# Mask rows moved from ScalarE to VectorE, and a new order of work in the gated-attention layer of an eight-layer kernel

## The reference

```python
# cross attention 0 and 3, masked
sim = jnp.where(mask[:, None, None, :], sim, max_neg)
attn = jax.nn.softmax(sim, axis=-1)
...
# feed-forward 0, "gated attention"; rw: [b, t, 16] gates from _gating
rw = _gating(hidden_states, sim_matrix, gates)
q = jnp.einsum('bte,bted->btd', rw, jnp.einsum('btc,ecd->bted', hidden_states, q_proj))
k = ...  # the same with k_proj
v = ...  # the same with v_proj
scores = jnp.where(causal, jnp.einsum('bqd,bkd->bqk', q, k) * scale, -jnp.inf)
attn = jnp.einsum('bqk,bkd->bqd', jax.nn.softmax(scores, axis=-1), v)
mixed = attn[:, :, None, :] * rw[..., None]
return jnp.einsum('bted,edc->btc', mixed, o_proj)
```

## Time and profile before

| what | us |
| --- | --- |
| median of 3 runs | 3174.82 |
| lowest, highest run | 3174.57, 3177.18 |
| the profiled execution, its own time | 3177.18 |
| its span in the profile | 3175.4 |
| layer 0 attention, about | 0 to 348 |
| gated attention, about | 348 to 965 |
| layer 3 attention, about | 2358 to 3055 |

### The profile page before, as it was taken

How to read it: one execution, slowest core, us unless ns; L and a number is a source line. 1 busy time by engine, 2 the same in 40 slices (tenths; PEclk the granted TensorE clock), 3 DMA queues, 4 the chain that set the end, 5 groups by cost and what they waited for, 6 DMA issues and landing times. The chain is left out here.

```text
span 3175.4 us, 91385 instructions
## 1 busy us (share of the span) xinstructions
PE 2974.0 (94%) x35250; PEld 2314.1 (73%) x35250; DVE 2237.6 (70%) x6007; ACT 1577.7 (50%) x2929; POOL 1200.9 (38%) x1402
## 2 busy tenths in 40 slices
PE   7999799999998999689988999999989999999978
PEld 6888455555557888556667888888877888888854
DVE  6777666666645666677777777777767777777755
ACT  6777221111215777366663333333336777677746
POOL 6776100000005776644430000000016676667643
PEclk9999899999998999989998999999999999999989
DMA  5000266656650000011103333323320000000001
GB/s 166 10 11 5 87 189 186 169 163 189 179 148 9 11 10 8 2 61 26 23 16 99 102 104 97 96 97 107 108 64 12 8 10 10 7 10 10 8 1 54
DMA packets 111033, 212.23 MB, mean 67 GB/s; under 512 B 18769, under 2 KB 30609, under 8 KB 110353
## 3 DMA queue, kind: packets, MB, share of 16 engines
q1 hardware_dynamic: 110352, 209.19, 22.4%
q10 hardware_dynamic: 512, 0.92, 0.1%
HBM read 198.50 MB, written 5.77 MB: 64 GB/s over the span
## 5 line engine op out<-in xcount | busy, mean ns | idle before, releaser
L349 PE MATMUL ps<-parts 128*128 128x512 f32 (+2 forms) x1568 | 624.0, 398 | 30.0 <-DVE parts L1014 18.3
L350 PE MATMUL ps<-parts 128*128 128x512 f32 (+2 forms) x1568 | 565.2, 360 | 0.0
L351 PE MATMUL ps<-parts 128*128 128x512 f32 (+2 forms) x1568 | 564.5, 360 | 0.0
L319 POOL TENSOR_TENSOR rstd<-mv,eps 128x4 f32<-128x4 f32 x112 | 23.2, 208 | 1220.2 <-DVE mv L302 1220.0
L1934 ACT ACTIVATE work<-ps 128x512 f32<-128x512 f32 x272 | 162.6, 598 | 455.0 <-PE ps L351 454.8
L349 PEld LDWEIGHTS ps<-parts 128*128 128x128 f32 (+1 forms) x1568 | 299.3, 191 | 101.0 <-ACT work L846 26.2
L351 PEld LDWEIGHTS ps<-parts 128*128 128x128 f32 (+1 forms) x1568 | 298.6, 190 | 47.3
L350 PEld LDWEIGHTS ps<-parts 128*128 128x128 f32 (+1 forms) x1568 | 300.7, 192 | 21.0
L562 POOL TENSOR_TENSOR work<-work 128x512 f32<-128x512 f32 x256 | 266.9, 1043 | 128.2 <-DVE work L984 128.2
L1900 PEld LDWEIGHTS ps<-early,work 128*128 128x128 f32 x2176 | 281.3, 191 | 30.2 <-DVE work L1991 11.4
L1900 PE MATMUL ps<-early,work 128*128 128x128 f32 x2176 | 289.0, 276 | 8.1 <-DVE x L2098 8.1
(11 more groups left out here) (297 smaller groups left out, 6259.6 us busy)
## 6 DMA issues: line engine op xcount, KB each, us to landing
work<-gate_rows SPq DMA_DIRECT2D x128, 512.0 KB, 5.6
work<-expert_rows SPq DMA_DIRECT2D x512, 128.0 KB, 2.9
work<-gate_rows SPq DMA_DIRECT2D x128, 256.0 KB, 7.1
work<-in_ctxT SPq DMA_DIRECT2D x72, 192.0 KB, 2.4
out<-x SPq DMA_DIRECT2D x16, 256.0 KB, 2.3
work<-work SPq DMA_DIRECT2D x224, 16.0 KB
work<-work SPq DMA_DIRECT2D x16, 128.0 KB, 2.3
early<-in_l0f_w SPq DMA_DIRECT2D x1, 1536.0 KB, 8.2
```

The lines of the kernel that those rows point to most:

```text
L349: T.matmul(out, lh, rh, start=True, stop=False)
L350: T.matmul(out, lh, rl, start=False, stop=False)
L351: return T.matmul(out, ll, rh, start=False, stop=True)
```

## The change

It has three parts. (1) `mask_rows` goes from ScalarE to VectorE, as a `tensor_scalar` of the same 128x256 values: for the first unit just ahead of the first `shift`, and for each next unit at step 2, between `sums` and `shift`. (2) In the loop of the gated layer, PE runs `router(g + 2)` in slot 1, ahead of `scores(g)`, not in slot 0, and `turn_gates(g + 2)` behind `project(g + 1, 5)` in slot 5, not behind `attend(g)` in slot 4. VectorE runs `weight` one slot ahead of PE, not two; `mask` and `normalise` come ahead of the `weight` of their slot; and the three batches of `routing(g + 2)` are in slots 2 to 4, not 1 to 3. In the prologue VectorE makes two products of group 0, not four, ahead of the routing of group 1; ScalarE's copy for `null_values` comes ahead of the first `gate_exp`, and `squares(1)` behind the copy for `spectral_weight`. (3) The gates go through two DRAM tensors in turn, not through one with a place for each group, and `rows_out` waits until the reads of two groups before have landed.

```diff
--- before.py
+++ after.py
@@ -862,10 +862,6 @@
                 act.wait_ge(sub_ready, n + 1)
                 A.activation(pr[t % 2], sc[t % 2], ACT.Exp, scale=1.0 if masked else scale).then_inc(exp_ready, 1)
 
-            def mask_rows(un):
-                tiles = mask[:, bass.ds(un.g * TG, TG), :]
-                A.activation(nm[un.u], tiles, ACT.Copy, bias=NEG, scale=-NEG).then_inc(nm_ready, 1)
-
             def weights_high(dst, src, parts):
                 for p in range(passes):
                     cols = slice(p * HP * DH, (p + 1) * HP * DH)
@@ -890,9 +886,6 @@
             if boot:
                 act.wait_ge(boot.ctx1, 16)
             A.activation(ch[1][0:DC, :], c.ctx01[0:DC, 0 if null else 1, :], ACT.Copy).then_inc(high, 1)
-            if masked:
-                act.wait_ge(mask_in, 16)
-                mask_rows(first)
             for j in range(NJ):
                 take_query(first, j, j % 2)
             if null:
@@ -923,9 +916,6 @@
                             A.activation(r0T[0:2 * HP, :], c.ps[0:2 * HP, 4, :], ACT.Copy).then_inc(r0t_ready, 1)
                         act.wait_ge(o_ready, n + 1)
                         A.activation(oT.rearrange("p j b q -> p b j q"), ps_o, ACT.Copy).then_inc(ot_out, 1)
-                        if masked and t == 0 and not end:
-                            need(act, s_read, n)
-                            mask_rows(un.next())
                         if turns(u, t, last):
                             take_hT(un.g + 1 if null else un.k + 2)
                         if not (end and t == TG - 1):
@@ -954,6 +944,10 @@
 
         @block.vector
         def _(ve):
+            def mask_rows(un):
+                tiles = mask[:, bass.ds(un.g * TG, TG), :]
+                V.tensor_scalar(nm[un.u], tiles, 1.0, -NEG, ALU.subtract, ALU.mult).then_inc(nm_ready, 1)
+
             def shift(n, un, t):
 
                 if masked and t == 0:
@@ -1036,6 +1030,9 @@
             context_low(second)
             ve.wait_ge(ht_full, 1)
             norm.scale(ve, 1)
+            if masked:
+                ve.wait_ge(mask_in, 16)
+                mask_rows(first)
             shift(0, first, 0)
             if null:
                 norm.take_moments(ve, 1, 1)
@@ -1064,6 +1061,8 @@
                             elif not (isinstance(it, int) and it == 0):
                                 add(it * 2 - 1)
                         if t < 2 or not end:
+                            if t == 2 and masked:
+                                mask_rows(un.next())
                             if boot and isinstance(it, int) and it == 0 and u == 0 and t == 3:
                                 ve.wait_ge(s_ready, n + 3)
                                 boot.vector_second(ve, c.ps[:, 3, S:S + NE0])
@@ -2139,7 +2138,7 @@
     ps_q, ps_v = [c.ps[:, i, :] for i in range(2)], [c.ps[:, 2 + i, :] for i in range(2)]
     ps_s, ps_m, ps_a, acc = (c.ps[:, 4 + i, :] for i in range(4))
     dup = c.w["dup"]
-    rows = nc.dram_tensor("gate_rows", [n * NE0, GT], FP).ap()
+    rows = [nc.dram_tensor(f"gate_rows{i}", [NE0, GT], FP).ap() for i in range(2)]
     norm = Norm(c, "f0_ln", hn)
     sem = lambda s: c.sem("f0_" + s)
     ht_full, ht_out, r_ready, r_read, n2_ready, rn_ready, gexp, rw_ready, link, wt_full, wt_out, rows_in = (
@@ -2161,21 +2160,23 @@
             def rows_out(g, u):
 
                 sp.wait_ge(wt_out, g + 1)
-                sp.dma_start(rows[bass.ds(g * NE0, NE0), :], rwT[u][0:NE0, :]).then_inc(rows_in, 16)
+                if not (isinstance(g, int) and g < 2):
+                    sp.wait_ge(split_in, (g - 1) * NM * 32)
+                sp.dma_start(rows[u], rwT[u][0:NE0, :]).then_inc(rows_in, 16)
                 sp.wait_ge(rows_in, g * 16 + 16)
 
             def spread_wide(g, u, p):
 
                 if not (isinstance(g, int) and g == 0 and p < NW):
                     sp.wait_ge(hw_ready, g * NP + (p - NW + 1) if p >= NW else g * NP - (NW - 1 - p))
-                sp.dma_start(wide[p % NW], rows[bass.ds(g * NE0 + 2 * p, 2), :].unsqueeze(0).broadcast_to((P, 2, GT))).then_inc(wide_in[p % NW], 16)
+                sp.dma_start(wide[p % NW], rows[u][2 * p:2 * p + 2, :].unsqueeze(0).broadcast_to((P, 2, GT))).then_inc(wide_in[p % NW], 16)
 
             def spread_split(g, u, i):
 
                 if not (isinstance(g, int) and g == 0):
                     sp.wait_ge(mixed_ready, g * NM - (NM - 1 - i))
                 for e in range(2):
-                    src = rows[bass.ds(g * NE0 + 4 * i, 4), :].rearrange("(j e) k -> e j k", e=2)[e:e + 1, :, :]
+                    src = rows[u].rearrange("(j e) k -> e j k", e=2)[e:e + 1, 2 * i:2 * i + 2, :]
                     sp.dma_start(split[i][e * DH:(e + 1) * DH, :, :], src.broadcast_to((DH, 2, GT))).then_inc(split_in, 16)
 
             sp.dma_start(dft, d["dft"]).then_inc(dft_in, 16)
@@ -2340,17 +2341,17 @@
                             project(g + 1, 1 - u, s)
                         if s == 0:
                             values(g)
-                            if left(g + 2):
-                                router(g + 2, u)
                         if s < 2 and left(g - 1):
                             back(g - 1, 2 + s)
                         if s == 1:
+                            if left(g + 2):
+                                router(g + 2, u)
                             scores(g)
                         if s == 3:
                             turn_probs(g)
                         if s == 4:
                             attend(g)
-                        if s == 4 and left(g + 2):
+                        if s == 5 and left(g + 2):
                             turn_gates(g + 2, u)
                         if s >= 6:
                             back(g, s - 6)
@@ -2402,13 +2403,13 @@
             take_hT(0, 0), squares(0)
             act.wait_ge(freq_full, 1)
             A.activation(freq.rearrange("p n w -> p (n w)"), c.ps[:, 4, 0:2 * P], ACT.Copy).then_inc(freq_out, 1)
-            gate_exp(0), take_gates(0, 0)
-            take_hT(1, 1), squares(1)
             act.wait_ge(nv_full, 1)
             A.activation(c.w["l3_nwo"][:, :, :].rearrange("p b c -> p (b c)"), c.ps[0:16, 7, 0:2 * D], ACT.Copy).then_inc(nv_out, 1)
+            gate_exp(0), take_gates(0, 0)
+            take_hT(1, 1)
             act.wait_ge(spec_full, 1)
             A.activation(c.w["l1f_g"][:, :], c.ps[:, 6, 0:P], ACT.Copy).then_inc(spec_out, 1)
-            gate_exp(1), take_gates(1, 1)
+            squares(1), gate_exp(1), take_gates(1, 1)
 
             def body(it):
                 for u in range(2):
@@ -2536,15 +2537,14 @@
                 routing(0, 0, part)
             ve.wait_ge(n2_ready, TG)
             norm.vector(ve, 1)
-            for p in range(NHW):
-                weight(0, 0, p)
+            weight(0, 0, 0), weight(0, 0, 1)
             for part in range(11):
                 routing(1, 1, part)
             ve.wait_ge(n2_ready, 2 * TG)
             norm.vector(ve, 2)
-            for p in range(NHW, NP):
+            for p in range(2, NP):
                 weight(0, 0, p)
-            weight(1, 1, 0), weight(1, 1, 1)
+            weight(1, 1, 0)
             ve.wait_ge(spec_out, 1)
 
             def body(it):
@@ -2555,18 +2555,18 @@
                             mix(g, s - 5)
                         if s == 0 and left(g - 1):
                             mix(g - 1, 3)
-                        if s < NP - 2 and left(g + 1):
-                            weight(g + 1, 1 - u, s + 2)
-                        if s >= NP - 2 and left(g + 2):
-                            weight(g + 2, u, s - NP + 2)
                         if s == 2:
                             mask(g)
                         if s == 3:
                             normalise(g)
+                        if s < NP - 1 and left(g + 1):
+                            weight(g + 1, 1 - u, s + 1)
+                        if s == NP - 1 and left(g + 2):
+                            weight(g + 2, u, 0)
                         if s == 2 and left(g - 1):
                             add(g - 1)
-                        if 1 <= s <= 3 and left(g + 2):
-                            for part in ((0, 1, 2, 3), (4, 5, 6, 7, 8), (9, 10))[s - 1]:
+                        if 2 <= s <= 4 and left(g + 2):
+                            for part in ((0, 1, 2, 3), (4, 5, 6, 7, 8), (9, 10))[s - 2]:
                                 routing(g + 2, u, part)
                         if s == 5 and left(g + 3):
                             ve.wait_ge(n2_ready, g * TG + 3 * TG)
```

## The result

The changed kernel takes 3207.65 us (median of four runs, 3204.94 to 3210.41), against 3174.9 for the kernel before beside it: a ratio of 1.0101, 95% interval 1.0087 to 1.0114. It is 32.7 us slower; the forecast was 17.4 us slower, with 3204 as its upper end. The profiled execution took 3206.64 us, with a span of 3204.3.

The account below looks back on a forecast made before the run. PE was taken to bound the kernel, with a 0.6 us wait per gated group. Mask rows +0.2, loop +9.8, prologue +4.4 and clock +3.0 sum to +17.4 us: 3192.2 us on the median, range 3179 to 3204.

Parts of the forecast that it names:

- I take 0, since a hold-up of up to 0.8 us fits into the cover.: Layers 0 and 3: GpSimd holding the mask rows costs nothing, as VectorE's L964 idled 1.20 us for the scores.
- The bound: Mask rows: held 1.27 us by GpSimd, they pass the cover by about 0.5, at most 24 us over 47 units.
- the shared port: Rival: GpSimd holds `mask_rows` past its cover, 47 x 0.2 to 0.5 us on top, about 3204; 8 in 100.
- The other terms: Gated layer: loop +9.8 us, prologue +4.4, lower clock after the prologue's idle time +3.0.
- The forecast's check on layers 0 and 3: Layers 0 and 3: windows with the same time, L964 still idle 0.7 to 0.9 us for PE.
- The loop: Gated loop: waits for product 4 (0.39 us) and `take_probs` (0.31) add 0.70 in each of 14 groups, +9.8.
- The prologue: Gated prologue: projection 2 starts 5.9 us later, less an old wait of 1.47, net +4.4 us on PE.
- The old wait of 1.47: Gated prologue: a PE wait at 387.67 in the earlier trace, forecast to go.
- lost to the clock: Gated prologue: after 4.4 us of PE idle time a lower granted clock costs +3.0 us, between 0 and 4.1.
- DMAs and queue: Gated loop: gates come 3.6 us later but with at least 1.3 us of cover, and SP's added wait costs nothing: 0.
- The wait simply goes: Rival: the 0.6 us wait at L2281 vanishes, 7.8 us come back, 3167 with a hidden prologue; 6 in 100.
- The even exchange: Rival: the loop's waits sum to the old 0.6 us, only a prologue of 4.4 is paid, 3179; 11 in 100.

Follow-up runs that it names:

- part 1 alone: Mask rows on VectorE at step 2, gated layer as before, against the kernel before: 3195.1 us against 3174.96, ratio 1.0062.
- only normalise first: Kernel before with `normalise` ahead of the product of its slot, products still two slots ahead: 3165.19 us against 3172.93, ratio 0.9974.
- the prologue alone: Kernel before with the new order in the gated layer's prologue only, its loop as before: 3179.89 us against 3172.93, ratio 1.0022.

## Why the prediction was wrong

**The step that failed: "I take 0, since a hold-up of up to 0.8 us fits into the cover."** The mechanism stood in the text, with the right pair of engines. Its size was taken from the earlier trace rows, as "about the length of a GpSimd operation, 1.27", with only L552 read beside the four instructions. The row that follows in the same timeline is

```profile
9.36 0.73 POOL L553 TENSOR_TENSOR parts<-parts,zero 96x256 fp32r<-96x256 f32 x1
```

and in the trace the four take 1.298, 0.767, 0.334 and 0.336 us: one is held to the end of L552, the next to the end of L553. So a hold by one GpSimd instruction at a time was a fair reading there, but the prediction did not look at what stands beside step 2. The trace of before had those rows too (the mask row would begin at about 183.1):

```profile
182.51 1.28 POOL L552 TENSOR_TENSOR parts<-parts,zero 96x512 fp32r<-96x512 f32 x1
183.75 0.73 POOL L553 TENSOR_TENSOR parts<-parts,zero 96x256 fp32r<-96x256 f32 x1
184.43 1.05 POOL L562 TENSOR_TENSOR work<-work 128x512 f32<-128x512 f32 x1
185.44 1.30 POOL L326 TENSOR_TENSOR x<-x,rows 128x512 f32 x1
```

Here the hold goes through three of them and lasts 2.55 us, and with 1.2 of cover gone PE waits 1.5. The bound, 47 units by 0.5 us, was wrong in both factors: the price is three times that, and only 13 units, all in layer 0, pay it. That its 24 us lie near the 18.2 measured (20.1 with part 1 alone) is luck. In layer 3 the mask rows looked at lie beside a GpSimd instruction on 128x4 elements that did not hold them: one began at 2603.4, beside L568 (2603.00, 1.02 us), and took 0.293 us. The rival "the shared port", with 8 in 100 and 3204 us, was the case that came, though it spread the hold over 47 units. The other terms, +17.2 by the forecast, measured +14.7 (7.8 and 6.9).

**The forecast's check on layers 0 and 3** ("windows with the same time") held in layer 3 within 1.2 us and failed in layer 0: L958 idles 0.19 us for L949, not 0.7 to 0.9 for PE.

**The loop: mechanism right, size 9.8 for 6.9.** Each of the three waits came in its place: 0.28 for `normalise` (forecast 0.35), 0.48 for product 4 (0.6), 0.17 for the copy behind `gate_exp` (0.31). A group costs 0.48 more, not 0.70; all three were sized a little long. The idle times alone sum to only 0.32 more than before (11.0 us in twelve groups against 7.2). A wait also costs the overlap between neighbouring matmuls: from the transposes to the projection it is 1.13 us from start to start with 0.48 of idle time (550.66 to 551.79), and 0.49 with none (450.22 to 450.71 in the kernel with only normalise first), so the distance of starts is the price. Putting the copy first took one of the waits away and left the others as they were, so they are separate.

**The prologue: right in its sum.** Counted from the first transposes, projection 2 is 6.5 us later (404.48 - 371.0 against 379.75 - 352.8; forecast 5.9). The first projection is 1.0 later (391.44 - 371.0 against 372.24 - 352.8; forecast 1.5), so the part that comes from the two products behind the routing is 5.5, not 4.4. The idle time is 4.52 us (4.4). The old wait of 1.47 is gone. From there to the gate transposes it is 8.71 us (404.48 to 413.19) against 5.85 before (379.75 in the earlier trace rows to 385.60, the row below), with PE busy throughout: 2.86 lost to the clock (3.0). Together 7.9; measured 7.8, and 8.0 with the prologue alone. DMAs and queue: PE has no wait for gates in the loop, as forecast.

```profile
385.60 0.60 PE L2245 MATMUL ps<-ident,work 128*16 128x128 f32 x4
```

**The rivals.** "The wait simply goes" did not come: product 4 (550.52) ended behind the transposes, and PE waited 0.48 for it. But what it rests on is sound: with `normalise` moved and the products left two slots ahead the whole wait goes, 8.5 us of the loop, somewhat more than 13 x 0.6, because a group gains 0.67. The even exchange fell, by 6.6 to 6.9 us of loop in three kernels.

## What to carry to other kernels

When an elementwise operation moves to VectorE beside a busy GpSimd, read GpSimd's timeline at that very place and reckon with the whole run of instructions that stand there without a pause, not with one: here the hold ended one, three or four instructions on, and no run shows a rule by which to tell. Then look for a step where it rests, or a form that runs at the plain rate: 0.49 us that nobody holds was better than 0.29 that became 2.55. When something urgent shares an in-order queue with something early, move the urgent one ahead by itself. The new loop also took a slot of lead from the early ones and moved the routing, and that turned one wait of 0.6 us into three that sum to 0.95 in the group shown. Which of its moves costs how much was not tried one by one; the longest wait, 0.48, is for the product that lost its lead.

## What the runs showed of the hardware that was not expected

- A held `tensor_scalar` gets its turn at some boundaries between GpSimd instructions and not at others. In layer 0 of the changed kernel 12 mask rows passed the boundaries from L552 to L553 and from L553 to L562 and got in where L326 begins; the one at 63.25 passed that one too, to the end of L326, and lasted 3.76 us. Yet in the earlier trace rows one got in just at L552 to L553 (8.19 + 1.30 = 9.49), and in layer 3 one got in behind a single GpSimd instruction (2431.4, 1.14 us). A register instruction of GpSimd's queue belongs to L326 in ten of the units, but at 298.40 and 319.40 there is none, and the mask row got in there as well, after 2.58 us. What decides stays open.
- The Trainium skill ("SBUF — State Buffer", Who interferes with whom) says that whoever issues first gets the pair for the whole instruction. By the starts in the trace the mask row at 192.35 would then have gone ahead of L553 at 193.00, and it did not. But the trace shows when GpSimd's instructions start and not when they are issued, so this case does not settle the rule.
- GpSimd hardly lost by it: the median of L552 in layer 0 was 1.279 us, before 1.277, and with part 1 alone that of L562 was 1.044, before 1.042. Only L326 rose, from a median of 1.297 to 1.372 us, which is where the mask row got in.
- Cutting a held instruction into four made it worse, 3.89 us instead of 2.55, as the second was held again.
